# One bias moved off TensorE in a fused vision-transformer block: ScalarE scales it, VectorE adds it during eviction

## What is computed

```python
for e in range(E):
    mid = jax.nn.relu(jnp.einsum('bsd,fd->bsf', x, W1[e]) + b1[e])
    ye = jnp.einsum('bsf,df->bsd', mid, W2[e]) + b2[e]
    out = out + w[..., e:e + 1] * ye
```

## Time and profile before

| | us |
|---|---|
| median of 3 runs | 2025.38 (2020.0 to 2028.93) |
| profiled execution | 2043.73 |
| its span | 2041.6 |

### The profile page before, as it was taken

One profiled execution on the slowest core, in us unless ns is written; L12 is line 12 of the kernel. 1 busy time (PEld: TensorE's weight loads), 2 busy tenths in 40 slices (PEclk: granted clock), 3 DMA queues, 4 the chain that ended last, 5 costly groups with the idle time before them and its releaser, 6 DMA issues. The chain is left out here.

```text
span 2041.6 us, 53942 instructions
## 1 busy us (share of the span) xinstructions
PE 1800.3 (88%) x17621; PEld 1314.0 (64%) x17621; DVE 1508.9 (74%) x4659; ACT 1277.0 (63%) x2661; POOL 1140.6 (56%) x1070
## 2 busy tenths in 40 slices
PE   4888988899898989888998339999999999999996
PEld 3666766666666766666665226676667677767775
DVE  4798889888988898889887356667666666774442
ACT  4788888888888888888888324444444444433332
POOL 4345464555555555555552355767767676765444
PEclk8998999999999899999998559999999999999998
DMA  4586665656566565656564558999999899988884
GB/s 156 145 254 195 185 207 168 197 181 187 179 186 194 174 185 180 194 174 186 179 176 124 126 135 211 209 234 201 224 218 223 218 214 230 200 206 191 183 191 79
DMA packets 401798, 382.70 MB, mean 187 GB/s; under 512 B 183796, under 2 KB 365360, under 8 KB 397552
## 3 DMA queue, kind: packets, MB, share of 16 engines
q1 hardware_dynamic: 359984, 338.67, 58.5%
q0 software_dynamic: 41664, 42.12, 12.3%
HBM read 223.20 MB, written 125.83 MB: 171 GB/s over the span
## 5 line engine op out<-in xcount | busy, mean ns | idle before, releaser
L2048 ACT ACTIVATE mh<-mid_bank 128x512 bf16<-128x512 f32 x336 | 200.7, 597 | 413.9 <-PE mid_bank L1642 337.1
L889 DVE TENSOR_REDUCE row_max<-s_bank 98x2 f32<-98x392 f32 x768 | 394.4, 555 | 53.3 <-PE s_bank L655 51.2
L1952 DVE SCALAR_TENSOR_TENSOR ml<-mid_bank,mh 128x512 bf16<-128x512 f32 x336 | 232.0, 691 | 257.4 <-ACT mh L2048 228.5
L1087 ACT ACTIVATE probs<-t_bank 98x392 f32<-98x392 f32 x768 | 339.7, 499 | 106.9 <-PE t_bank L671 104.3
L2121 POOL DMA_INDIRECT out_rows<-y_out,tail x168 | 268.9, 1601 | 146.3 <-DVE y_out L1986 103.8
L1656 PE MATMUL y_bank<-wst,mh 128*128 128x192 bf16 x1344 | 329.9, 245 | 10.9 <-DVE y_out L1986 9.7
L1659 PE MATMUL y_bank<-wst,ml 128*128 128x192 bf16 x1344 | 330.0, 246 | 0.0
L1658 PE MATMUL y_bank<-wst,mh 128*128 128x192 bf16 x1344 | 329.7, 245 | 0.2 <-issue 0.2
L655 PE MATMUL s_bank<-k_stack,q_stack 96*98 96x196 f16 x1536 | 234.5, 259 | 47.3 <-DVE row_max L889 34.1
L1263 POOL TENSOR_TENSOR x_lo<-x_buf,x_hi 128x588 f16<-128x588 f32 x128 | 170.4, 1343 | 177.2 <-DVE x_b L954 73.0
L671 PE MATMUL t_bank<-q_stack,k_stack 104*98 104x196 f16 x1536 | 225.1, 259 | 35.7 <-ACT probs L1087 32.7
(11 more groups left out here) (264 smaller groups left out, 4397.4 us busy)
## 6 DMA issues: line engine op xcount, KB each, us to landing
wst<-packed SPq DMA_DIRECT2D x56, 1584.0 KB
x_buf<-in_x_t SPq DMA_DIRECT2D x32, 1176.0 KB, 7.9
q_stack<-stack_parts SPq DMA_DIRECT2D x288, 98.0 KB, 2.5
k_stack<-stack_parts SPq DMA_DIRECT2D x288, 98.0 KB, 2.6
stack_parts<-qk_hi SPq DMA_DIRECT2D x32, 588.0 KB, 2.8
stack_parts<-qk_lo SPq DMA_DIRECT2D x32, 588.0 KB, 3.1
out_rows<-h_buf SPq DMA_DIRECT2D x32, 294.0 KB
h_in<-out_rows SPq DMA_DIRECT2D x32, 294.0 KB
```

The lines of the kernel that those rows point to most:

```text
L889: nc.vector.reduce_max(row_max[st.odd][:, :, hh:hh + 1], s_bank[hh % 2][0:HALF, :, 0:TOKENS], AX.X).then_inc(max_ready, 1)
L1087: nc.scalar.activation(probs[st.odd][:, hh], t_bank[hh % 2][0:HALF, :, 0:TOKENS], ACT.Exp).then_inc(probs_ready, 1)
L1952: nc.vector.scalar_tensor_tensor(ml[n % MID][:], mid_bank[n % MID_PS][:], 0.0, mh[n % MID][:], ALU.max, ALU.subtract).then_inc(ml_ready, 1)
L2048: nc.scalar.activation(mh[n % MID][:], mid_bank[n % MID_PS][:], ACT.Relu).then_inc(mh_ready, 1)
```

## The change

- The bias columns of `packed` double: each row of a half expert now holds half of the second bias in float32 (192 columns of 2 bytes), the same in all 128 rows. `packed`, `pack` and `wst` are typed as 16-bit words and read as bfloat16, float16 or float32.
- `split_biases` scales the second bias instead of splitting it (7 steps instead of 12). One fill of zeros goes; the two stores of the second bias now spread it over 128 rows.
- The four bias matmuls and `three` go. The sums rotate over three banks (`y_at`): a tile takes the bank that is free and then the one after it.
- TensorE waits for the evictions twice, ahead of quarter 0 (all of the tile before the last one, since that bank was its second) and ahead of quarter 2 (the first two of the last tile). It signals `y_half` after quarter 1 of the sixth chunk.
- ScalarE evicts nothing. At the end of a tile's turn, behind the copy of `xe` for the next tile, it multiplies the bias by the four gates into `gated_b2` (`gate_bias`).
- VectorE evicts all four quarters with one operation each: sum times gate, plus `gated_b2`.
- SP waits for `bias_gated` too before it loads weights into a buffer.

```diff
-BIAS_COLS = DIM // 2
+BIAS_COLS = DIM
...
-                    zeros = blank[:, 0:BIAS_COLS].bitcast(BF16).unsqueeze(1).to_broadcast([P, 2 * EXPERTS, BIAS_COLS])
-                    sp.dma_start(packed[:, :, PACK - BIAS_COLS:].rearrange("h p n -> p h n"), zeros
-                                 ).then_inc(bias_zeroed, 16)
...
                 for t in range(2):
-                    sp.dma_start(packed.rearrange("(e t) p n -> e t p n", t=2)[:, t, 0:3, PACK - BIAS_COLS:],
-                                 b2_split[:, :, t * BIAS_COLS:(t + 1) * BIAS_COLS]).then_inc(bias_stored, 16)
+                    half = DIM // 2
+                    sp.dma_start(packed.rearrange("(e t) p n -> e t p n", t=2)[:, t, :, PACK - BIAS_COLS:].bitcast(F32),
+                                 b2_scaled[:, t * half:(t + 1) * half].unsqueeze(1).to_broadcast([EXPERTS, P, half])
+                                 ).then_inc(bias_stored, 16)
...
+        gated_b2 = sb("gated_b2", [P, TJ, DIM])
...
-        y_bank = [ps(f"y_bank{i}", [P, 2, 256]) for i in range(2)]
+        y_bank = [ps(f"y_bank{i}", [P, 2, 256]) for i in range(3)]
...
+        def y_at(i, j):
+
+            return y_bank[(2 * i + j // 2) % 3][:, j % 2, 0:DIM]
...
+                wait(sp, bias_gated, TJ * (i - DEEP + 1))
                 sp.dma_start(wst[q][:], packed.rearrange("(e t) p n -> e t p n", t=2)[bass.ds(e, 1)]
...
-                if c == 0:
-                    wait(pe, evicted, TJ * i)
...
                 for j in range(TJ):
                     cols = slice(j * P, (j + 1) * P)
-                    o = y_bank[j // 2][:, j % 2, 0:DIM]
+                    o = y_at(i, j)
+                    if c == 0 and j % 2 == 0:
+                        wait(pe, evicted, TJ * (i - 1) + j)
...
-                if c == FCH - 1:
-                    for j in range(TJ):
-                        last = nc.tensor.matmul(y_bank[j // 2][:, j % 2, 0:DIM], three[:],
-                                                wst[q][:, :, PACK - BIAS_COLS:], start=False, stop=True,
-                                                skip_group_check=True)
+                    if c == FCH - 1 and j == 1:
+                        last.then_inc(y_half, 1)
                 last.then_inc(used, 1)
...
             def evict(i):
                 q = i % 2
-                dve.wait_ge(used, FCH * (i + 1))
+                dve.wait_ge(bias_gated, TJ * (i + 1))
                 dve.wait_ge(gate_step, gate_steps(i + 1))
                 wait(dve, added, 16 * TJ * (i - 1))
-                for j in (2, 3):
-                    nc.vector.tensor_scalar(y_out[q][:, j, :], y_bank[j // 2][:, j % 2, 0:DIM], gate[q][:, j:j + 1],
-                                            None, ALU.mult).then_inc(evicted, 1)
+                for j in range(TJ):
+                    if j == 0:
+                        dve.wait_ge(y_half, i + 1)
+                    elif j == 2:
+                        dve.wait_ge(used, FCH * (i + 1))
+                    nc.vector.scalar_tensor_tensor(y_out[q][:, j, :], y_at(i, j),
+                                                   gate[q][:, j:j + 1], gated_b2[:, j, :], ALU.mult, ALU.add
+                                                   ).then_inc(evicted, 1)
...
-            def evict(i):
+            def gate_bias(i):
                 q = i % 2
-                act.wait_ge(used, FCH * (i + 1))
                 act.wait_ge(gate_step, gate_steps(i + 1))
-                wait(act, added, 16 * TJ * (i - 1))
-                for j in (0, 1):
-                    nc.scalar.mul(y_out[q][:, j, :], y_bank[j // 2][:, j % 2, 0:DIM], gate[q][:, j:j + 1]
-                                  ).then_inc(evicted, 1)
+                wait(act, evicted, TJ * i)
+                b2_row = wst[i % DEEP][:, :, PACK - BIAS_COLS:].bitcast(F32)
+                for j in range(TJ):
+                    nc.scalar.mul(gated_b2[:, j, :].rearrange("p (t n) -> p t n", t=2), b2_row, gate[q][:, j:j + 1]
+                                  ).then_inc(bias_gated, 1)
...
-                    elif c == 1:
-                        if tile_there(i - 1):
-                            evict(i - 1)
...
                     elif c == 5:
                         copy_edge(i + 1)
+                        if tile_there(i):
+                            gate_bias(i)
```

More of the change, by code:

```diff
@@ L256, in attention_phase @@
         b2_rows = sb("b2_rows", [EXPERTS, DIM])
-        b2_rest = [sb(f"b2_rest{i}", [EXPERTS, DIM]) for i in range(3)]
-        b2_split = sb("b2_split", [EXPERTS, 3, DIM], BF16)
+        b2_scaled = sb("b2_scaled", [EXPERTS, DIM])
         s_bank = [ps(f"s_bank{i}", [P, 2, 256]) for i in range(2)]
@@ L855, in split_biases @@
                 dve.wait_ge(bias_in, 32)
[L856 to L864, removed]
+                op(nc.vector.tensor_scalar(b1_rest[0][:], b1_rows[:], W_SCALE, None, ALU.mult), 1)
+                op(nc.vector.tensor_copy(b1_split[:, 0], b1_rest[0][:]), 2)
+                op(nc.vector.tensor_tensor(b1_rest[1][:], b1_rest[0][:], b1_split[:, 0], ALU.subtract), 3)
+                op(nc.vector.tensor_copy(b1_split[:, 1], b1_rest[1][:]), 4)
+                op(nc.vector.tensor_tensor(b1_rest[2][:], b1_rest[1][:], b1_split[:, 1], ALU.subtract), 5)
+                op(nc.vector.tensor_copy(b1_split[:, 2], b1_rest[2][:]), 6)
+                op(nc.vector.tensor_scalar(b2_scaled[:], b2_rows[:], W_SCALE, None, ALU.mult), 7)
             def low_part(body):
@@ L1180, in high_part @@
                 else:
-                    nc.scalar.copy(pack[:, W1_COLS:W1_COLS + W2_COLS], stage_2[:]).then_inc(w_hi_ready, 1)
+                    nc.scalar.copy(w2_pack[:, 0:W2_COLS], stage_2[:]).then_inc(w_hi_ready, 1)
             def fill_pipeline():
@@ L1441, in expert_phase @@
         instead = sb("instead", [P, REST, TJ], I32)
-        wst = [sb(f"wst{i}", [P, 2, PACK], BF16) for i in range(DEEP)]
+        wst = [sb(f"wst{i}", [P, 2, PACK], U16) for i in range(DEEP)]
         xT = [sb(f"xT{i}", [P, 3, T], F16) for i in range(DEEP)]
@@ L1494, in expert_phase @@
         added = sem("added")
+        bias_gated = sem("bias_gated")
+        y_half = sem("y_half")
         number_ready = sem("number_ready")
@@ L1498, in expert_phase @@
         spares_ready = sem("spares_ready")
-        CONSTS = 5
+        CONSTS = DEEP
         ROUTE = 11
@@ L1658, in project @@
                     nc.tensor.matmul(o, mh[n % MID][:, cols], low, start=False, stop=False, skip_group_check=True)
[L1659 removed]
+                    last = nc.tensor.matmul(o, ml[n % MID][:, cols], high, start=False, stop=(c == FCH - 1),
                                             skip_group_check=True)
[L1661 to L1665 removed]
+                    if c == FCH - 1 and j == 1:
+                        last.then_inc(y_half, 1)
                 last.then_inc(used, 1)
@@ L1691, in _ @@
                 nc.vector.memset(row[s][:, :, XROW:ROW], 0.0).then_inc(rows_set, 1)
-            nc.vector.memset(three[:], 0.0).then_inc(consts_set, 1)
             for i in range(DEEP):
@@ L1697, in _ @@
             nc.vector.tensor_copy(taken[:], first_slot[:])
-            dve.wait_ge(consts_set, 4)
-            nc.vector.memset(three[0:3, :], 1.0).then_inc(consts_set, 1)
             def route(g):
```

20 lines of the change are left out of this document (9 added, 11 removed).

## The result

| | before | after | ratio, 95% interval |
|---|---|---|---|
| first comparison, median us | 2025.61 | 2044.3 (2041.66 to 2046.97, 4 runs) | 1.0091, 1.0063 to 1.012 |
| again on another chip, median us | 2023.26 | 2048.62 (2046.05 to 2056.74, 6 runs) | 1.0137, 1.0115 to 1.0159 |

The change costs 18.7 us in one comparison and 25.4 in the other; why the second gave more isn't known. The forecast was 2026.0 with a range of 2007 to 2039: wrong, and on the side to which it gave 17%.

The account below looks back on a forecast made before the run. Routed tiles: TensorE and a two-tile loop nearly balanced; last stage: GpSimd and DMA. +0.5, -1.0 (first three tiles) and +1.1 (last stage) make +0.6 on 2043.73: 2044.3, or 2026.0 at the median's 0.9% difference; range 2007 to 2039 us.

Parts of the forecast that it names:

- The step from the profile to the time: Whole kernel: profiled execution 2043.73 us, timed median 2025.38, 0.9% below; the same difference turns 2044.3 into 2026.0.
- What bounds the routed tiles: Tiles 3 to 41, 14.82 us each: TensorE and a two-tile loop nearly balanced, the transpose landing 0.6 us ahead of need.
- The stall of 0.34 us: Routed tiles, ahead of the first `y_bank` matmul: TensorE waits for the eviction; the change should remove this 0.34 us.
- The eviction: End of a tile: VectorE's four in a row take 1.38 us, ending 0.43 us later (0.2 to 0.7) in routed tiles.
- The loop leads nearly always: Routed tiles after the change: the two-tile loop gives 14.83 us a tile, TensorE's own turn 14.1; +0.5 us over 39 tiles.
- ScalarE's scalings, the new wait of SP: Behind the copy of `xe`: four scalings take 1.4 to 2.2 us, costing nothing or a few tenths; SP's wait costs nothing.
- The load: Weight load per tile, 1584 to 1632 KB: +0.2 us in the loop (0 to +0.5), about 0.1 in 13 last-stage rounds.
- The last stage: Last fourteen tiles, GpSimd's additions and their DMA landings: together +1.1 us, between -1 and +3.
- The set-up: Attention phase: a zero fill goes, two later stores of 384 KB come, five VectorE steps go; 0, at most +3 us.
- A: Rival, routed tiles: TensorE's saving comes through, 14.17 us a tile, -25 us, 2000 us; chance of over 10 us gained 0.2.
- B: Rival, two-tile loop: serial eviction and heavier load lengthen it, +14 us, 2039 us; chance of over 10 us lost 0.17.
- C: Rival, routed tiles: TensorE's stall stays at VectorE's second quarter, unseen; 2026 to 2028 us, sharing 0.63 with the forecast.

Follow-up runs that it names:

- narrow: Kernel after, with the second bias stored from 128 partitions and held as 16-bit floats, so a tile's load is 1584 KB: 2030.81 us, 1.0037 against before.
- narrow, nothing added: "narrow" with the second bias left out: ScalarE scales nothing, VectorE still evicts all four quarters from three banks; 2032.14 us, 1.0063 against before.
- the base: Kernel before without its four bias matmuls a tile, the second bias left out of the result: 2022.92 us, again 2021.04 us.

## Why the prediction was wrong

- *The step from the profile to the time.* The text noted that the profiled execution was 0.9% above the median and let "the same difference" stand. That was the first fault. That execution had late notices, a stall in 20 tiles and a period of 14.82; the two others of before that were profiled, which lie in the timed range, have none of these, and neither has after. Against the profile it argued from, the sum looks close, +0.6 us forecast and +3.2 measured, but that is luck. From the start to tile 3's copy it forecast -1.0 and +3.6 came, for the routed tiles +0.5 and -6.7 came (563.8 to 557.1), for the last stage +1.1 and +6.7 came (211.9 to 218.6). Against the two usual profiles the three are about +5, +11 and +4.5.
- *What bounds the routed tiles.* "TensorE and the loop are nearly balanced" held, but not with the numbers given. In the two usual executions TensorE's own turn is 14.14 us, not 14.48, and `xe` waits for `xT` in only 13 and 14 of 39 tiles, 8.6 and 11.8 us in all. The stall of 0.34 us that the change was to remove did not exist in them.
- *The eviction.* The best step. Forecast 3 x 0.32 + 0.42 = 1.38 us; measured 1.38. Forecast end 0.43 later; measured 5.98 - 5.54 = 0.44, and GpSimd's sends 18.60 - 18.17 = 0.43 later. "The loop leads nearly always" came true: 18 waits in the trace of after, about one in each pair of tiles. The period is 14.66, forecast 14.83.
- *ScalarE's scalings, the new wait of SP.* Forecast 1.4 to 2.2 us and nothing on the path; measured 1.49 (1582.16 to 1583.65 in tile 23), the first chunk half a microsecond later, and nothing on the path that "narrow" against "narrow, nothing added" could show.
- *The load.* Forecast 0.2 in the loop and 0.1 in each of 13 rounds, some 5 us in all if both counted. Measured alone 3.4 and 6.4 us, too rough to judge the size; by the profiles more of it lies in the last stage.
- *The last stage.* +1.1, between -1 and +3; measured about +4.5. A faster TensorE doesn't help: the base, too, took 217.0 us. Mis-sized: the load weighs more there than 0.1 a round (218.6 to 220.2 us with it against 212.5 to 213.5 without, serial eviction in all), and the later eviction, out of three banks, shows no weight there (213.5 us on the base).
- *The set-up.* "0, at most +3"; measured 8.6 alone and 10 in the change. This was the second fault. The step counted bytes and a landing time from a fill that comes from 128 partitions, and named nothing queued behind the two stores on SP, though their source has 8 partitions. Behind them stood the next image's loads. "It is one time, in the attention phase, far ahead of the wait at its end" was the wrong step: the wait that counts is GpSimd's for `h_in`, 14.6 us, directly behind.
- *The rivals.* A was wrong: TensorE stands 28 us in the routed tiles of after. Its doubt was sound, though: the long notice was no fixed price, and as it is gone in before too, it favours neither kernel. B had the right place (end of eviction, additions, sends, transpose) and the right sign, 2039 us by its own sum; it did not have the store. C's stall indeed hardly mattered, since there was none.

## What to carry to other kernels

Before arguing from a trace, hold the profiled execution against the range of the timed ones; if it lies outside, the balance that it shows between two nearly equal limits is not the balance of the runs that count. Where two limits lie within a few tenths of a microsecond, work taken off the one is worth almost nothing, and a delay on the other costs its full share: here 0.33 us a tile off TensorE brought 2 us, and 0.65 later in the eviction, on a loop over two tiles, cost 9. Price a one-time store by what is queued behind it and by where it comes from, not by its bytes alone: here 768 KB from 8 partitions cost 9 to 10 us.

## What the runs showed of the hardware

- 2 x 384 KB in pieces of 384 bytes from 8 partitions held SP's queue: the issues took 5.42 us, the next one 7.95 us, with 48 GB/s moved. The same bytes from 128 partitions, in one transfer: 0.41 and 1.85 us.
- A wait of TensorE of 2.85 us in a stretch otherwise full was followed by half the clock for 3.4 us (1.2 GHz instead of 2.4), which made that wait cost some 1.7 us more. Windows of after, tile 23 (a DMA share above 1 is how the view prints it in windows this short):

```profile
1564.00:1566.00 2.00, 0.00 (x0) 0.00 (x0) 1.50 (x13) 0.00 (x0) 1.39 (x2) 1.00 1.17 213
1566.00:1568.00 2.00, 1.52 (x5) 0.62 (x6) 0.00 (x0) 1.59 (x5) 1.69 (x2) 0.74 1.11 310
1568.00:1570.00 2.00, 2.00 (x13) 1.79 (x12) 0.94 (x4) 1.05 (x4) 0.38 (x2) 0.50 0.95 201
1570.00:1572.00 2.00, 2.00 (x20) 1.28 (x18) 0.31 (x2) 0.51 (x1) 0.00 (x0) 0.90 0.98 410
```

  It happened twice in the routed tiles of this profile, behind waits of 2.09 and 2.85 us, and neither in those of the second profile of after nor in before's three.
- One execution of an unchanged program had notices of TensorE's matmuls 1.2 to 1.4 us later than two others in chunk 1 of its routed tiles (medians), and 16 to 19 us more in those tiles, at a full clock.
